# Two sets of weights loaded under the layer before, and composed inside the third layer's program

## The reference

```
x = layernorm(x + L0(x, adj))      # softmax over j of sum_c relu(fa_i + fb_j) * W2
x = layernorm(x + L1(x, adj))      # the same with a leaky relu, then a linear layer
x = layernorm(x + L2(x, adj))      # s = x @ W1 + b1; f1 = s @ a1 + ba1; f2 = s @ a2 + ba2
                                   # softmax down the columns of leaky(f1_j + f2_i), mask; elu(coefs @ s)
x = layernorm(x + L3(x, adj))      # 8 heads: q, k, v, edge bias by type, leaky, mask, softmax, @ Wp + bp
```

## Time and profile before

| | us |
|---|---|
| median of 3 runs | 5830.69 (5829.75 to 5830.9) |
| profiled execution, its own time | 5828.89 |
| span of the profiled execution, first to last instruction | 5826.4 |
| PE busy in the span | 5530.6 (95%) |
| DVE busy | 5404.7 (93%) |
| ACT busy | 5129.8 (88%) |
| POOL busy | 906.6 (16%) |
| mean granted TensorE clock, as a share of 2.4 GHz | 0.967 |

### The profile page before, as it was taken

One profiled execution on the slowest core, in us unless ns is written; L12 is line 12 of the kernel. 1 busy time (PEld: TensorE's weight loads), 2 busy tenths in 40 slices (PEclk: granted clock), 3 DMA queues, 4 the chain that ended last, 5 costly groups with the idle time before them and its releaser, 6 DMA issues. The chain is left out here.

```text
span 5826.4 us, 138045 instructions
## 1 busy us (share of the span) xinstructions
PE 5530.6 (95%) x58164; PEld 2225.6 (38%) x58164; DVE 5404.7 (93%) x8136; ACT 5129.8 (88%) x6073; POOL 906.6 (16%) x889
## 2 busy tenths in 40 slices
PE   8999999999999999999999999997778889888888
PEld 2333333333333333333333333333444445444444
DVE  8999999999999999999999999996768899889988
ACT  8999999999999999999999999985858888888887
POOL 0000000000000111111211111111302222222223
PEclk9999999999999999999999999997879999999999
DMA  1000000000000000000000000002511111011100
GB/s 42 19 19 20 16 19 19 19 16 19 19 19 16 19 19 16 19 19 16 19 19 16 19 16 19 19 12 82 150 38 28 32 32 32 25 32 32 35 22 18
DMA packets 144490, 156.45 MB, mean 27 GB/s; under 512 B 51782, under 2 KB 119110, under 8 KB 143878
## 3 DMA queue, kind: packets, MB, share of 16 engines
q1 hardware_dynamic: 143238, 147.55, 9.1%
q10 hardware_dynamic: 640, 0.07, 0.0%
HBM read 137.10 MB, written 2.10 MB: 24 GB/s over the span
## 5 line engine op out<-in xcount | busy, mean ns | idle before, releaser
L323 DVE TENSOR_SCALAR a_hidden<-a_B,a_A 128x1024 f32<-128x1024 f32 x4992 | 3592.2, 793 | 85.1 <-PE apsS L214 66.0
L249 ACT ACTIVATE a_hidden<-a_B,a_A 128x1024 f32<-128x1024 f32 x3200 | 3424.5, 1139 | 200.7 <-PE apsS L214 197.0
L214 PE MATMUL apsS<-a_hidden,a_w_sel 128*32 128x512 f32 x32768 | 3560.3, 593 | 11.4 <-DVE a_hidden L323 11.2
L214 PEld LDWEIGHTS apsS<-a_hidden,a_w_sel 128*32 128x32 f32 x32768 | 1044.4, 110 | 2424.5 <-issue 2036.1
L652 PE MATMUL m3S<-xT,Q 64*128 64x512 f32 x2048 | 615.0, 674 | 90.9 <-ACT x_even L696 61.9
L696 ACT ACTIVATE x_even<-m3S,bias 128x512 f32<-128x512 f32 x684 | 433.2, 687 | 209.2 <-PE m3S L652 184.8
L668 PE MATMUL m3O<-ZT,Xr 32*64 32x256 f32 x16384 | 573.5, 411 | 4.3 <-DVE ZT L745 4.3
L668 PEld LDWEIGHTS m3O<-ZT,Xr 32*64 32x64 f32 x16384 | 356.4, 142 | 326.5 <-issue 240.0
L745 DVE STREAM_TRANSPOSE ZT<-x_even 128x1024 f32<-128x1024 f32 x342 | 422.4, 1238 | 57.9 <-ACT x_even L705 53.2
L736 DVE CUSTOM_DVE_ANT_0 x_even<-x_even,mask 128x1024 f32<-128x1024 f32 x342 | 428.8, 1289 | 38.5 <-ACT x_even L696 38.4
L705 ACT ACTIVATE x_even<-x_even,low 128x1024 f32<-128x1024 f32 x342 | 393.7, 1151 | 0.0
(11 more groups left out here) (157 smaller groups left out, 3180.4 us busy)
## 6 DMA issues: line engine op xcount, KB each, us to landing
a_adj_in<-adj SPq DMA_DIRECT2D x128, 512.0 KB, 3.6
adj_in<-adj SPq DMA_DIRECT2D x128, 512.0 KB, 4.0
Xr<-x_odd SPq DMA_DIRECT2D x128, 64.0 KB, 3.0
out<-yn SPq DMA_DIRECT2D x64, 32.0 KB, 1.5
x_even<-x SPq DMA_DIRECT2D x1, 256.0 KB, 2.9
wqT<-L_wqT SPq DMA_DIRECT2D x1, 130.0 KB, 2.6
wkT<-L_wkT SPq DMA_DIRECT2D x1, 130.0 KB, 2.7
wvT<-L_wvT SPq DMA_DIRECT2D x1, 130.0 KB, 2.8
```

The lines of the kernel that those rows point to most:

```text
L214: last = pe.matmul(psS[k % 2][32 * q:32 * q + 32, h * HALF:(h + 1) * HALF], w["sel"][layer][:, 30 - 2 * p:62 - 2 * p], hidden[:, (k * GROU ...
L249: act.activation(hidden[:, (k * GROUPS + p) % SLOTS, q, :], B2[:, g % 2, :], ACT.Relu, bias=A2[:, g % 2, pair:pair + 1]).then_inc(hid_act, 1)
L323: dve.tensor_scalar(hidden[:, (k * GROUPS + p) % SLOTS, q, :], B2[:, g % 2, :], A2[:, g % 2, pair:pair + 1], 0.0, ALU.add, ALU.max).then_i ...
```

## The change

The seven arrays of the third layer get buffers that live beside those of the first two layers, and SP loads them in `additive_layers` behind tile 4. `ba` is cleared in the first block with the other zeros. The six arrays of the fourth layer get buffers in the third layer, and SP loads them in `column_layer` behind tile 8, and the first tile of `adj` for the heads layer behind the last tile. The blocks `zero_bias`, `load_weights` (both) , `column_constants` and `heads_constants` are gone. What they computed is now part of `column_layer`: the third layer's part ahead of its loop, with the row of ones set by POOL, and the fourth layer's part in the last steps of the loop, on PE in steps T, T+1, T+2, T+4 and T+6.

```diff
@@ additive_layers, SP
+                if k == 4:
+                    for dst, src in later:
+                        sp.dma_start(dst, src).then_inc(later_loaded, 16)
+            sp.wait_ge(later_loaded, 16 * len(later))
@@ column_layer, PSUM places
+        ps1, ps2 = psR[1][0:W, 0:1], psR[1][0:W, HALF:HALF + P]
+        psQ, psV, psK = psA[0:C, 0, :], psA[:, 1, :], psR[0][:, HALF:HALF + C]
+        psC, psB, psE = psR[0][:, 0:PAIRS], psR[0][0:C, HEADS:2 * HEADS], psR[0][:, 2 * HEADS:3 * HEADS]
@@ column_layer, SP
+                if k == 8:
+                    for dst, src in later:
+                        sp.dma_start(dst, src).then_inc(later_loaded, 16)
+            sp.dma_start(adj_in3, adj[0:P, :]).then_inc(adj_loaded3, 16)
@@ column_layer, POOL
+            gp.memset(xT[C:W, :, :], 1.0).then_inc(ones_ready, 1)
+            gp.wait_ge(ones_ready, 1)
@@ column_layer, PE
+            COMPOSED_IN = {0: (0, 1), 1: (2,), 2: (3, 4), 4: (5,), 6: (6, 7)}
+            def compose():
+                pe.matmul(ps1, w["w1T"], w["a1"], start=True, stop=True)
+                pe.wait_ge(a2_spread, 1)
+                pe.matmul(ps2, w["w1T"], w["a2B"], start=True, stop=True).then_inc(composed, 1)
+            def compose_head(h):
+                if h == 0:
+                    pe.wait_ge(later_loaded, 16 * len(later))
+                    pe.wait_ge(biases_spread, 2)
+                    pe.wait_ge(seq_out, nb)
+                    pe.wait_ge(neg_ready, nb - 1)
+                    pe.wait_ge(pos_ready, nb - 1)
+                pair, e = divmod(h, 2)
+                side = slice(C * e, C * e + C)
+                pe.matmul(psQ[:, h * C:(h + 1) * C], wqT[:, h, 0:C], wkT[:, h, 0:C], start=True, stop=True)
+                for g in range(2):
+                    pe.matmul(psV[C * g:C * g + C, h * C:(h + 1) * C], wvT[:, h, 0:C], wp[:, h, :], start=True, stop=True)
+                pe.matmul(psC[side, pair:pair + 1], wkT[:, h, 0:C], wqT[:, h, C:C + 1], start=True, stop=True)
+                pe.matmul(psB[:, h:h + 1], wqT[:, h, 0:C], wkT[:, h, C:C + 1], start=True, stop=True)
+                pe.matmul(psE[:, h:h + 1], bqB[:, h, :], wkT[:, h, C:C + 1], start=True, stop=True)
+                pe.matmul(psK, bvB[:, h, :], wp[:, h, :], start=h == 0, stop=h == HEADS - 1).then_inc(heads_made, 1)
@@ spread_f2, first graph
+                    pe.wait_ge(w_ready, 2)
+                    pe.wait_ge(ones_ready, 1)
@@ PE's program
             turn_x(0)
+            compose()
             spread_f2(0)
...
+                if i - T in COMPOSED_IN:
+                    for h in COMPOSED_IN[i - T]:
+                        compose_head(h)
@@ column_layer, DVE
+            def keep_heads():
+                dve.wait_ge(heads_made, HEADS)
...
+            dve.tensor_copy(w["a2B"], w["a2"].to_broadcast([C, P])).then_inc(a2_spread, 1)
+            dve.tensor_tensor(fold, ident[:, 0:C], ident[:, C:P], ALU.add)
+            dve.wait_ge(composed, 1)
+            dve.tensor_scalar(w["seq"][:, C:W], ps1, w["ba"][:, 0:1], None, ALU.add).then_inc(w_ready, 1)
+            dve.tensor_scalar(w["f2"], ps2, w["ba"][:, 1:2], None, ALU.add).then_inc(w_ready, 1)
...
+                if i == 4 * tiles + 6:
+                    spread_biases()
+                if i == T + tiles + 3:
+                    keep_heads()
@@ heads_layer, SP
-            load(0)
             load_rows(0)
```

More of the change, by code:

```diff
@@ L41, in dve_made, with additive_layers @@
     return 4 * (g + 1) - act_made(g)
-def additive_layers(nc, adj, X, rest, w, buf, small, ident, nb, n):
+def additive_layers(nc, adj, X, rest, later, w, buf, small, ident, nb, n):
     tiles = n // P
@@ L485, in heads_layer @@
-def heads_layer(nc, adj, out, w, X, buf, small, ident, nb, n):
+def heads_layer(nc, adj, out, w, X, buf, adj_loaded, small, ident, nb, n):
     tiles = n // P
@@ L872, in build @@
                       (beta[:, :], a["L1_gnn_beta"].to_broadcast([P, 1])), (ycol[:, :], a["L1_gnn_yita"])]
-            load_constants(nc, loads, more, [w_sel[0][:, :], w_sel[1][:, :], w_a[0][:, :, :], w_a[1][:, :, :]], ident[:, :],
+            load_constants(nc, loads, more, [w_sel[0][:, :], w_sel[1][:, :], w_a[0][:, :, :], w_a[1][:, :, :],
+                                       ba[:, :]], ident[:, :],
                            identb[:, :], small)
@@ L877, in build @@
             additive_constants(nc, w, ycol[:, :])
-            additive_layers(nc, adj, X, x_rows(tiles, nb * tiles), w, buf, small, ident[:, :], nb, n)
+            additive_layers(nc, adj, X, x_rows(tiles, nb * tiles), later, w, buf, small, ident[:, :], nb, n)
         cur = 0
@@ L890, in build @@
                        vare=sg("vare2", [P, tiles])[:, :], rstd=sg("rstd2", [P, tiles])[:, :])
[L891 to L900 removed]
+            w = dict(seq=w_seq[:, :], f2=w_f2[:, :], w1T=w1T[:, :], a1=a1[:, :], a2=a2[:, :], a2B=a2B[:, :], ba=ba[:, :])
+            column_layer(nc, adj, w, w3, raw, later, adj_in3[:, :], adj_loaded3, X[0], X[1], buf, small, ident[:, :],
+                         identb[:, :], nb, n)
         if stages == 3:
@@ L928, in build @@
                        rstd=sg("rstd3", [P, 1])[:, :])
-            heads_layer(nc, adj, out, w, X[1], buf, small, ident[:, :], nb, n)
-def load_weights(nc, name, loads, spread=()):
-    with ExitStack() as ctx:
-        loaded = ctx.enter_context(nc.semaphore(name + "_loaded"))
-        block = ctx.enter_context(nc.Block())
-        @block.sync
-        def _(sp):
-            for dst, src in loads:
-                sp.dma_start(dst, src).then_inc(loaded, 16)
-            sp.wait_ge(loaded, 16 * len(loads))
-        @block.vector
-        def _(dve):
-            dve.wait_ge(loaded, 16 * len(loads))
-            for dst, src in spread:
-                dve.tensor_copy(dst, src)
+            heads_layer(nc, adj, out, w3, X[1], buf, adj_loaded3, small, ident[:, :], nb, n)
 def store_rows(nc, X, out, tiles):
@@ L986, in host_arrays, with column_layer @@
     return r
-def column_layer(nc, adj, w, X, XN, buf, small, ident, identb, nb, n):
+def column_layer(nc, adj, w, w3, raw, later, adj_in3, adj_loaded3, X, XN, buf, small, ident, identb, nb, n):
     tiles = n // P
@@ L1281, in _ @@
                     negative_exp(b - 2)
-def zero_bias(nc, ba):
-    with ExitStack() as ctx:
-        block = ctx.enter_context(nc.Block())
-        @block.vector
-        def _(dve):
-            dve.memset(ba[:, :], 0.0)
-def column_constants(nc, w, buf, ident, a1, a2B, w1T, ba):
-    W = C + 1
-    with ExitStack() as ctx:
-        ps1 = ctx.enter_context(nc.psum_tensor("c2w1", [W, HALF], F32))
-        ps2 = ctx.enter_context(nc.psum_tensor("c2w2", [W, HALF], F32))
-        composed = ctx.enter_context(nc.semaphore("c2composed"))
-        block = ctx.enter_context(nc.Block())
-        @block.tensor
-        def _(pe):
-            pe.matmul(ps1[:, 0:1], w1T, a1, start=True, stop=True).then_inc(composed, 1)
-            pe.matmul(ps2[:, 0:P], w1T, a2B, start=True, stop=True).then_inc(composed, 1)
-        @block.vector
-        def _(dve):
-            dve.memset(buf["xT"][C:W, :, :], 1.0)
-            dve.tensor_tensor(buf["fold"], ident[:, 0:C], ident[:, C:P], ALU.add)
-            dve.wait_ge(composed, 2)
-            dve.tensor_scalar(w["seq"][:, C:W], ps1[:, 0:1], ba[:, 0:1], None, ALU.add)
-            dve.tensor_scalar(w["f2"], ps2[:, 0:P], ba[:, 1:2], None, ALU.add)
 def kernel(**inputs):
```

107 lines of the change are left out of this document (40 added, 67 removed).

## The result

| | before | changed |
|---|---|---|
| median of the runs on one chip, us | 5830.55 (5828.54 to 5834.64, 6 runs) | 5805.43 (5803.24 to 5807.35, 6 runs) |
| profiled execution, its own time, us | 5828.89 | 5804.34 |

What follows compares the result with a forecast made beforehand. PE, DVE and ACT were taken as near full, leaving two seams (9.05 and 21.93 us) as the prize. Terms -8.4 - 17.0 + 0.7 = -24.7 us, from a median of 5830.69, gave 5806; 8-in-10 range 5797 to 5812.

Steps and rivals of the forecast that it cites:

- First seam: Between x_even's last write and the column layer: PE's turn 8.75 us earlier, about 0.3 given back, net gain 8.4 us.
- Second seam, the removal: Between x_odd's end and PE's first heads-layer matmul: shrinks from 21.93 to 0.30 us, 21.6 us gained.
- Second seam, the price: At the column layer's end: composing heads between weighings delays x_odd 4.1 us, plus 0.5 for a clock fall; 4.6 us.
- PE's new timetable in the old trace's time: Column layer's end: heads at about 0.92 us and weighings at 1.9 put the last weighing 4.6 us later.
- rival B: Column layer's end: clock falls or copies and heads 6 and 7 don't fit; delay 8 to 12 us; chance 0.14.
- What followed for the seam: Second seam's net: 21.6 us removed less 4.6 us of delay, 17.0 us gained.
- The heads layer: No gain or loss counted inside the heads layer; an earlier first adj tile was costed at nothing.
- the forecast's own signs of being wrong: Heads layer's first 50 us not at clock 0.50, column loop off over 2 us, or POOL load waits near tiles 9 to 11.
- rival A: Heads layer gets the higher clock sooner: score steps save 5.5 us, work ahead 4.4; time 5796 to 5801; chance 0.18.
- Column loop: Inside the column layer: two DVE bias copies in step 38, bounds 0 and 1.4 us, taken as 0.7 us.
- The late tile: Column layer, tile 9: load 3 to 3.6 us late, covered by 4.9 us slack; costed at nothing, upper bound 3 us.
- DVE's copies: Column layer's end: seven copies, 1.83 us, fit in DVE's 2.11 us wait for POOL; uncovered, up to 1.8 us would show.

Runs made afterwards that it cites:

- second_seam: The kernel before with only the fourth layer's half of the change: its six arrays loaded early and composed in the column layer; 5813.61 us, ratio 0.9978.
- second_bank: The changed kernel with the heads' small results in psR[0]'s second bank, so head 0 doesn't wait, and the bias row's matmuls behind head 7; 5801.28 us.
- bank_again: second_bank run again, unaltered; 5800.07 us in one run.
- both delays: second_bank with one or three idle DVE copies behind the last normalisation (delay_one, delay_three); 5801.95 us in one run and 5802.6 us.
- keep_busy: second_bank with eight idle PE matmuls of 512 columns behind the composed heads at the column layer's end; 5806.16 us, ratio 0.996.
- spaced: second_bank with head 3 alone behind the last weighing, heads 4 to 7 behind the last fold, bias row's matmuls ahead of head 2; 5796.13 us.
- again_b: The changed kernel profiled again, unaltered; 5808.09 us in one run.
- wait_alone: The kernel before with only head 0's waits added at their place in PE's program, composing nothing there; 5833.38 us in one run.
- delay_one: second_bank with one idle DVE copy behind the last normalisation, to start the heads layer later; 5801.95 us in one run.
- delay_three: second_bank with three idle DVE copies behind the last normalisation, to start the heads layer later; 5802.6 us, ratio 0.9957.

## Why the prediction was right

The time was forecast at 5806 and measured at 5805.4. By its own steps it was less exact than that: two misses of opposite sign, 7.5 us too little cost and 6.3 us too little gain, nearly cancel. That the total is off by less than 1 us is luck.

- **First seam, -8.4.** Right. PE's turn starts 8.58 us earlier, spreading f2 8.25 us earlier and 3.33 us behind the turn (forecast 3.34). POOL's memset took 1.80 us where 2.1 was assumed from a slower row, and is hidden.
- **Second seam, the removal, -21.6.** Right: 0.32 us are left of 21.93.
- **Second seam, the price, +4.6 (4.1 by the timetable at `x_odd`, and 0.5 for the chance of a fall).** Wrong: +12.1. The step that failed is "PE's new timetable in the old trace's time", which took each head at 0.92 us and each weighing at 1.9. Its order of events is what the trace shows, its durations are not. Heads 0 and 1 took 3.72 us (4225.49 to 4229.21) for 1.84, the weighing 3.6 for 1.9, heads 2 to 4 5.7 for 2.8, the last weighing 3.3 for 1.9: 7.9 us more, so the last result is copied 12.6 us later relative to the positive part, of which 0.5 us of slack takes a part, as forecast. This is rival B at a price of 12.1, just above its 8 to 12, and above the 11 us given as the case in which all of it runs at 1.2 GHz: a head then took 1.9 us, not the 1.65 of the old block. At 2.4 GHz it took 1.1 (second_seam, heads 2 to 4 in 3.3 us), not 0.92, so the term was some 0.9 us short even without a fall. The forecast had head 0's wait in its timetable (heads from 4233.5, where the weighing ahead of them ended at 4229.56, see the row below), but drew nothing from this pause of 3.9 us for the clock; it weighed only whether narrow work lowers it. All four profiles with this wait and the composition have the fall at it and a tail of 25.7 to 28.0 us. The six in which head 0 doesn't wait but stands in the same place (second_bank, bank_again, both delays, keep_busy, spaced) have heads 0 and 1 at 2.4 GHz and a tail of 15.8 to 17.8.
- **What followed for the seam.** Net 21.6 - 12.1 = 9.5 us instead of 17.0.
- **The heads layer, 0.** Wrong: -6.3. The clock in the layer's first 50 us was not 0.50 throughout, one of the forecast's own signs of being wrong. Of these 4.9 are rival A's mechanism in part. (The pause of 14.6 us that was named for A stands ahead of the old composition; ahead of the layer itself PE paused 2.17 us, and now 5.79.) The score steps between 4271.3 and 4282.8 took 2.3 us (4276.01 to 4278.20, 4280.58) with PE at 1.13 instead of 2.08 us and ACT busy 8.61 of 9.00 us, where a step took 2.9 before; five of them gave 3.2 us, and the rise at 4292.5, ahead of the first weighing instead of behind it, 1.7 more. The layer's start and first scores stayed at 1.2 GHz, so it isn't the full 10 us of rival A. The last 1.4 us are behind the start of the first weighing. That weighing itself took 1.98 us, where it took 2.80 with the clock rising inside it, so 0.8 are the clock's again; the rest is within the 1507.3 to 1509.0 us (one 1511.2) that this part takes from kernel to kernel.
- **Column loop, +0.7.** +0.2 in the first profile and within the scatter in the others. The late tile is there: POOL waits for loads of `adj` inside the loop, 13.1 us in 11 waits (fence below) against 1.2 in 3 before, 9.4 of it from tile 8 to tile 14 (in again_b all such waits are 3.5 us in 5). The forecast had them as a sign of being wrong, but they cost nothing: the first graph took 41.27 us, before 41.65. PE's slack of 4.9 us covers the longest of them, 3.5.
- **DVE's copies.** Right: they stand from 4248.95 to 4250.62 inside the wait for POOL, which has 0.53 us left.

The weighing of the kernel before behind which head 0 now stands, from its timeline:

```profile
4227.62 1.94 PE L1101 MATMUL c2R<-Y,scaled 128*64 128x512 f32 x8
```

The view of waits of the changed kernel inside the loop (who waited for what, us in total, times, the longest):

```profile
POOL maskb L990 <- DMA adj_in<-adj: 13.1, 11, 3.5
```

Sum in measured terms, from the cuts: -8.3 at the first maximum, +0.2 in the loop, +12.1 in the tail, -21.6 in the seam, -4.9 in the scores, -1.4 behind, together -23.9 us of span. B and A were given 0.14 and 0.18 as alternatives, each with the other absent. They came together, and the time fell between them.

The Trainium skill (TensorE: Matmul & The Clock Gate, Part 1) has the clock rise after some microseconds of sustained matmuls. The changed kernel disagrees for narrow ones with two weighings among them: PE was busy 15.51 of 16.00 us at 1.2 GHz. keep_busy agrees with it for wide ones, since there the clock rose 4.6 us into the 512-column matmuls, with PE busy 4.50 of 4.50 us on heads at 1.2 GHz ahead of them, and so does second_seam, where it rose at the end of a weighing of 3.7 us. By that rule alone the composition would soon have been back at 2.4 GHz and the tail near 21 us, an estimate from the 15.8 before, the 4.1 of the forecast and the 1.1 of wait_alone; the 27.9 measured decide.

What stays open: what sets the early rise in the heads layer. In every kernel without idle matmuls that has it the rise is 18.8 to 20.2 us behind the layer's first matmul, in or just behind the layer's first gapless run of score and query matmuls. The kernel before has the same run (4287.5 to 4291.2) and no rise. The early stretch lasts 0, 3.4, 6.8 or about 10.2 us, and the scores then take 34.9, 34.1, 32.3 or 30.0 us. The changed kernel has about 10 in three profiles of three, second_bank's program 0 in one and 6.8 in another. Neither the start of the layer nor the pause ahead of it was shown to decide it. Open too is what makes the clock fall behind heads 2 to 4 in some profiles (bank_again, delay_one, second_seam) and not in others (second_bank, keep_busy, delay_three), and how long it then stays low.

## What to carry to other kernels

Work that is put into a gap of a tuned chain should not bring a wait of its own: look which buffer it writes, and who last reads that buffer. A pause of PE of 4 us cost about a microsecond where wide weighings followed, and 9 to 11 where narrow matmuls did (tails of 25.7 and 27.9 against 16.9). When a forecast sums terms at one clock, ask for each term what PE did in the microseconds ahead of it, and check a right total by its terms: this one was right with two terms off by 7.5 and 6.3 us.
